# Normalised tokens of the later rounds made on VectorE instead of GpSimd, in both mixtures of experts

## What is computed

```python
x = w_norm * (xf * rsqrt(mean(xf * xf) + EPS))
logits = x @ w_router                    # 32 experts
w_topk, sel = top_k(softmax(logits), 4)
# each expert: up to 128 tokens in order; buf[e] = x[tok]
y = (silu(buf @ w_gate) * (buf @ w_up)) @ w_down
out[tok] += y[...] * w_topk
sh = sigmoid(x @ w_shared_gate) * (silu(x @ sw_gate) * (x @ sw_up) @ sw_down)
return inp + out + sh
```

## Time and profile before

| | |
|---|---|
| median of three runs | 2836.43 us (2834.74 to 2837.26) |
| profiled execution, its own time | 2849.46 us |
| span of the profiled execution | 2847.7 us |
| mean granted TensorE clock | 0.957 |
| busy: TensorE, VectorE, ScalarE, GpSimd | 92%, 65%, 45%, 30% |
| first mixture, from the start to the last marks | 1366 to 1536 us of the span |
| second mixture, the same stretch | 2457 to 2620 us |
| chain that ended last, by engine | TensorE 12%, VectorE 1%, DMA 1%, the rest under 1% |

### The profile page before, as it was taken

The page is one execution under the profiler, slowest core; times in us unless marked ns, Lnnn a source line. Parts: engine busy times, 40 slices in busy tenths (PEclk is TensorE's granted clock), DMA queues, the critical chain, the costliest instruction groups (busy, mean ns, idle before and its releaser), DMA issues. The chain is left out here.

```text
span 2847.7 us, 38702 instructions
## 1 busy us (share of the span) xinstructions
PE 2633.2 (92%) x14106; PEld 1258.1 (44%) x14106; DVE 1857.3 (65%) x3962; ACT 1268.9 (45%) x1936; POOL 850.1 (30%) x820
## 2 busy tenths in 40 slices
PE   4887999999999999788799998899999999899998
PEld 2443233333333332344465664344455454465665
DVE  6556988887877887366465334877767677366334
ACT  3332366656656667634221231255555555521221
POOL 2655032241331400166432441212111110153441
PEclk8897799999999999999899999799999999999999
DMA  3004312303303210000411663632334340301565
GB/s 122 1 1 99 51 36 39 62 18 56 60 20 51 43 26 2 1 1 1 141 34 39 146 156 97 122 55 54 57 63 63 62 68 2 111 17 50 124 161 156
DMA packets 162592, 175.76 MB, mean 62 GB/s; under 512 B 19090, under 2 KB 135762, under 8 KB 162258
## 3 DMA queue, kind: packets, MB, share of 16 engines
q1 hardware_dynamic: 146948, 152.57, 24.4%
q0 software_dynamic: 12416, 17.84, 3.8%
q10 hardware_dynamic: 3040, 2.88, 0.4%
HBM read 116.32 MB, written 56.13 MB: 61 GB/s over the span
## 5 line engine op out<-in xcount | busy, mean ns | idle before, releaser
L1853 DVE TENSOR_REDUCE a_mx<-a_bank 128x1 f32<-128x512 f32 (+3 forms) x1792 | 1035.6, 627 | 260.9 <-PE a_bank L1587 180.3
L1723 ACT ACTIVATE a_E<-a_bank 128x1024 f32<-128x1024 f32 (+3 forms) x896 | 796.0, 931 | 457.8 <-PE a_bank L1644 311.6
L1587 PE MATMUL a_bank<-a_KT,a_QT 96*128 96x512 bf16 (+4 forms) x1792 | 592.4, 376 | 26.6 <-DVE a_mx L1853 17.0
L1644 PE MATMUL a_bank<-a_QT,a_KT 99*128 99x512 bf16 (+4 forms) x1792 | 506.9, 358 | 4.2 <-DMA a_QT<-a_mT 2.3
L1659 PE MATMUL a_bank<-a_E,a_Vg 128*32 128x512 f32 (+3 forms) x3584 | 437.3, 560 | 0.7 <-ACT a_E L1723 0.7
L1587 PEld LDWEIGHTS a_bank<-a_KT,a_QT 96*128 96x128 bf16 (+1 forms) x1792 | 151.8, 98 | 516.5 <-DVE a_mx L1853 326.0
L1644 PEld LDWEIGHTS a_bank<-a_QT,a_KT 99*128 99x128 bf16 (+1 forms) x1792 | 170.3, 98 | 173.8 <-ACT a_E L1723 30.9
L1020 ACT ACTIVATE d_silu<-d_bank 128x512 f32<-128x512 f32 x96 | 57.2, 596 | 351.3 <-PE d_bank L894 345.6
L447 POOL TENSOR_TENSOR f_hl<-f_hT,f_hh 128x512 f16<-128x512 f32 x96 | 110.6, 1156 | 336.8 <-ACT f_hh L464 336.3
L1101 DVE SCALAR_TENSOR_TENSOR d_silu<-d_silu,d_bank 128x512 f32<-128x512 f32 x96 | 65.8, 685 | 202.7 <-ACT d_silu L1020 202.6
L909 PE MATMUL d_bank<-wdT,d_hT 128*128 128x256 f32 (+1 forms) x768 | 194.0, 396 | 4.2 <-DVE d_hT L1104 4.2
(11 more groups left out here) (243 smaller groups left out, 3775.6 us busy)
## 6 DMA issues: line engine op xcount, KB each, us to landing
parts<-a_parts SPq DMA_DIRECT2D x64, 384.0 KB, 2.6
a_QT<-parts SPq DMA_DIRECT2D x180, 128.0 KB, 5.7
a_KT<-parts SPq DMA_DIRECT2D x180, 128.0 KB, 8.9
d_wgu<-in_L_ffn_w_gate SPq DMA_DIRECT2D x64, 176.0 KB
d_wgu<-in_L_ffn_w_up SPq DMA_DIRECT2D x64, 176.0 KB
d_wd<-in_L_ffn_w_down SPq DMA_DIRECT2D x64, 176.0 KB
normalised<-d_xn SPq DMA_DIRECT2D x8, 1152.0 KB, 4.7
acc<-d_zero SPq DMA_DIRECT2D x2, 4224.0 KB, 15.8
```

Of the source, the lines that this page charges most:

```text
L1587: last = nc.tensor.matmul(out[:, 0:w], QT[0:W, h, qt * P:(qt + 1) * P], KT[0:W, h, kh * HALF:kh * HALF + w], start=True, stop=not diag)
L1644: last = nc.tensor.matmul(out, KT[:, h, kt * P:(kt + 1) * P], QT[:, h, half * HALF + c0:(half + 1) * HALF], start=True, stop=not diag)
L1723: nc.scalar.activation(E[:, u % 2, 2 * pair:2 * pair + 2, c0:HALF], bank[:, 2 * pair:2 * pair + 2, c0:HALF], ACT.Exp).then_inc(exps, 1)
L1853: nc.vector.tensor_reduce(mx[:, x[1] // C % 2, j, qt, kh:kh + 1], out[:, 0:w], AX.X, ALU.max).then_inc(freed_dve, 1)
```

## The change

The normalise function goes from GpSimd's program to VectorE's and takes the round as an argument; the two buffer waits go with it. Round 0 stays ahead of the slots. The tiles of round c + 1 are made in the slots of chunk c: tiles 0 to 2 in slot 1, 3 to 5 in slot 3, 6 and 7 in slot 4, each time behind the routing step of that slot and ahead of `spot`. GpSimd keeps `mark` alone. No sum or product changes.

```diff
@@ -787,15 +787,6 @@
                                                  in_=ys[:, e % 2, :], in_offset=None, compute_op=ALU.add,
                                                  bounds_check=NTOK + TRASH - 1, oob_is_err=True).then_inc(added, 16)
 
-                def normalise(r, i):
-
-                    t = r * RT + i
-                    if r > 1 and i == 0:
-                        pool.wait_ge(turned, START + (r - 1) * (RT // 2))
-                        pool.wait_ge(xn_sent[r % 2], START + 16 * (r // 2))
-                    nc.gpsimd.tensor_scalar(xn[:, r % 2, i, 0:D], core.x[:, t, :], core.mv[:, t, 0:1], both[:, t:t + 1],
-                                            ALU.subtract, ALU.mult).then_inc(normed, 1)
-
                 def mark(r):
 
                     pool.wait_ge(masked, START + r + 1)
@@ -807,18 +798,8 @@
                         last = nc.gpsimd.tensor_scalar(marks[:, 0, i], hot[:, i], core.const("token_hi")[:, t:t + 1], None, ALU.mult)
                     last.then_inc(marked, 1)
 
-                pool.wait_ge(normed, START + RT)
-                pool.wait_ge(scales, START + 5)
-                for i in range(RT):
-                    normalise(1, i)
                 for r in range(NS):
-                    if r + 2 < NS:
-                        for i in range(RT // 2):
-                            normalise(r + 2, i)
                     mark(r)
-                    if r + 2 < NS:
-                        for i in range(RT // 2, RT):
-                            normalise(r + 2, i)
                 pool.wait_ge(zeroed, START + 16 * 2)
                 for s in range(2):
                     pool.wait_ge(xn_sent[s], START + 16 * (NS // 2))
@@ -1087,9 +1068,13 @@
                 scale_step(nc.vector.reciprocal(both[:], both[:]))
                 scale_step(nc.vector.tensor_tensor(both[:], both[:], core.rstd[:], ALU.mult))
 
-                def normalise(i):
-
-                    nc.vector.tensor_scalar(xn[:, 0, i, 0:D], core.x[:, i, :], core.mv[:, i, 0:1], both[:, i:i + 1],
+                def normalise(r, i):
+
+                    t = r * RT + i
+                    if r > 1 and i == 0:
+                        dve.wait_ge(turned, START + (r - 1) * (RT // 2))
+                        dve.wait_ge(xn_sent[r % 2], START + 16 * (r // 2))
+                    nc.vector.tensor_scalar(xn[:, r % 2, i, 0:D], core.x[:, t, :], core.mv[:, t, 0:1], both[:, t:t + 1],
                                             ALU.subtract, ALU.mult).then_inc(normed, 1)
 
                 def hidden(c, j):
@@ -1234,7 +1219,7 @@
                     last.then_inc(stats, 1)
 
                 for i in range(RT):
-                    normalise(i)
+                    normalise(0, i)
                 nc.vector.memset(zero[:], 0.0).then_inc(cleared, 1)
                 scale_step(nc.vector.tensor_scalar(keep[:], core.rstd[:], 0.5, 1.0, ALU.mult, ALU.add))
                 scale_step(nc.vector.tensor_tensor(shift[:], core.rstd[:], core.mv[:, :, 0], ALU.mult))
@@ -1260,6 +1245,9 @@
                                 carry(c)
                         if j == 5:
                             locate(c)
+                    if c < NS - 1 and j in (1, 3, 4):
+                        for i in {1: (0, 1, 2), 3: (3, 4, 5), 4: (6, 7)}[j]:
+                            normalise(c + 1, i)
                     if 0 < c < NS and j in (0, 1):
                         spot(c - 1, j)
                     if c == NS - 1 and j == 5:
```

## The result

The changed kernel takes 2880.61 us (median of four runs, 2873.84 to 2882.6) against 2836.85 us for the kernel before (four runs): a ratio of 1.0152 with a 95% interval of 1.0133 to 1.0170, 43.8 us slower. Measured once more on another occasion (experiment e9) the ratio is 1.0123, interval 1.0101 to 1.0145. The forecast was 2868 us in a range of 2857 to 2881. The direction and the places of the waits were right, and the size stands at the very edge of the range. 2880.61 is held here against 2836.85; in e9 the kernel before had a median of 2841.09 us, so the change cost 35 to 44 us.

A forecast was written before the change was run, and what follows sets the result against it. TensorE was taken to bound the kernel, with GpSimd's normalising covered. Waits of 19.2 + 7.7 - 0.9 = 26.0 us plus 6 us of clock made 32 us on the 2836.43 us median: 2868 us, range 2857 to 2881.

The forecast's parts named there:

- What bounds: Both mixtures' dense slots: TensorE sets the pace, GpSimd's normalising is already covered; its removal gives only -0.9 us.
- Pair 1: Second transpose pair, slot 3: waits for the fourth tile behind the choice, 4.25, 2.68, 2.68 us per mixture, 19.2 in both.
- Pair 3: Last transpose pair: waits for tiles 6 and 7 behind mask, sums and carry, 1.28 us each, 7.7 us in all.
- the slow carry: VectorE's carry in slot 4 takes 0.60 us beside GpSimd's marks, assumed in every round, instead of 0.19.
- Sum of the waits: Both mixtures: 19.2 + 7.7 - 0.9 = 26.0 us of TensorE waiting, 23.5 with the fast carry.
- The clock: TensorE falling to a lower clock level after new waits: three falls at 2.1 us, +6 us, bounds -3 to 15.8.
- the whole-instruction lock: Rival: VectorE's carry waits out a whole GpSimd marks instruction, 11.3 us more, about 2880 us; chance 0.05.
- six falls and 2878 us: Rival: the clock falls after all six new pair 1 waits, 26.0 + 15.8, 2878 us; chance 0.08.
- swallowed mask wait: Rival: slot 5's present mask waits vanish into the new wait, 7.1 us less, 2855 us without clock; chance 0.09.
- Faster: Rival: GpSimd's normalising keeps TensorE's short waits and clock falls alive; 18.4 us loss goes, about 2817 us; chance 0.02.
- no change: Rival: the order does not come out as written, TensorE never waits, only 0.9 us is left; chance 0.02.
- doubled mode for fp32 tensor_scalar: Skill rule for VectorE's normalise: would shorten the pair 1 and pair 3 waits by 2 us in all; not adopted.

The follow-up runs named there:

- e9: The changed kernel unaltered, measured again on another occasion: 2879.53 us, ratio 1.0123 to the kernel before.
- e1: Changed kernel with the fourth tile normalised in slot 1 instead of slot 3: 2847.95 us, ratio 1.0030 to the kernel before.
- e2: Changed kernel with tiles 6 and 7 normalised in slot 3 instead of behind the carry in slot 4: 2862.77 us, ratio 1.0084.
- e5: Changed kernel with extra useless TensorE products ahead of pair 1's wait, four in round 1's transposes, two in rounds 2 and 3: 2871.61 us, ratio 1.0118.
- e4: Changed kernel with extra useless TensorE products ahead of pair 1's wait, eight in round 1's transposes, five in rounds 2 and 3: 2877.34 us, ratio 1.0151.
- e10: e6 with one more extra product ahead of each pair 1 wait (five in round 1's transposes, three in rounds 2 and 3): 2869.59 us, ratio 1.0097.
- e6: e5 with one extra product ahead of each pair 3 wait as well: 2873.0 us, ratio 1.0132.

## Why the prediction was right, and where it was off

**What bounds.** That TensorE sets the pace and that GpSimd's normalising was covered held: with it gone, the only wait on TensorE that got shorter is that for the mask of round 1, from 0.94 to 0.48 us, where 0.45 us off was forecast. The marks' wait stayed at 3.06 us, as forecast, since no normalise stood ahead of it.

**Pair 1.** Forecast 4.25 and 2.68 us of delay. From the row in front of them to the transposes it is 5.96 us (1386.69 to 1392.65) where it was 1.71, and in round 1 it is 5.63 where it was 2.97: 4.25 and 2.66 us. (The idle time is 4.08 and 2.60, as one product overlapped the next at the old place.) Right in both sizes, and e1 shows the cause: one tile moved ahead of the choice and the wait is gone.

**Pair 3.** Forecast 1.28 us with the slow carry, 0.87 with the fast one; measured 1.11 to 1.21 us of idle time in the first mixture (0.93 once in the second), 1.27 us in TensorE's starts in round 1, with the carry at 0.59 us in every round. Taking the slow carry was right, and e2 shows the cause.

**Sum of the waits.** 26.0 us forecast. The first part of span x clock is 24.0 us above the kernel before in e9; in the four runs of the result it is 2748.9 us, 24 to 25 above the kernel before on the other occasions. Right.

**The clock.** This is the term that was mis-sized: I took +6 us, and the second part rose by 12.5 us in e9 (by up to 17 if its 129 us are held against the groups of the other occasions). The step that failed is the count: "three falls at 2.1 us, the trace's own frequency". Both profiles of the changed kernel lose 11 to 13 us more inside the two mixtures than before, and both show it at the same six places: behind four of the six waits for pair 1 (rounds 0 and 1, not round 2), and in round 0 of both mixtures behind the mask and pair 3. That makes about 2 us a place, so the price of 2.1 us was right and the number was not.

The count went wrong twice. I held only new waits of over 2 us to be worth one. But behind the mask of round 0, where the kernel before has a fall in one mixture alone, the changed one has it in both, and for longer: the dense rows take 3.62 and 2.67 us. Pair 3's 1.21 us stand less than 1 us behind the mask's 2.12, with only the mask's small products between them. With either kind of wait alone the fall at this place is shorter (3.56 and 1.88 us in e2, 3.33 and 1.88 in e5, and alike in their second mixtures). The losses in the table point the same way: 4.1 us above the kernel before in e1 and 3.1 in e2, together less than the 11 to 13 of both kinds. That they strengthen each other is suggested by one profile of each, and not shown.

And the frequency, two of four, left out three waits of over 2 us in the trace of the kernel before, those for transfers at the start of the mixtures:

```profile
1369.83 3.67 PE L846 MATMUL d_bank<-consts,d_xn 128*128 128x128 f32 x16 [5.41 <-DMA d_wr<-in_L_ffn_w_shared_gate]
...
1377.03 3.78 PE L894 MATMUL d_bank<-d_xT,wgT 128*128 128x512 f32 x4 [3.53 <-DMA wdT<-in_L_ffn_sw_down]
...
2460.57 3.42 PE L846 MATMUL d_bank<-consts,d_xn 128*128 128x128 f32 x16 [6.34 <-DMA d_wr<-in_L_ffn_w_shared_gate]
```

Behind all three the granted clock was 0.50. Five of seven would have made four falls of six and 9 us, by my estimate, and 2871 us in all.

How much of the surplus hangs on TensorE being idle is shown in part: filling the waits took 8 to 14 us off the loss in the two mixtures in four traces, and the totals of e4 and e10 agree; those of e5 and e6 show less.

**The range and the nearest rivals.** The result lies 0.4 us inside the upper end of 2881, and that end has no sum behind it: 41.8 us of waits and six falls make 2878, half of the lock's 11.3 us on top would make 2884. That the time fell inside is luck in part. The rival nearest to the time, the whole-instruction lock with about 2880 us, is wrong: the carry of round 0 (1403.31) took 0.59 us beside a GpSimd instruction that ran from 1402.76 for 2.85. The next, six falls and 2878 us, had the number of places right, but named the six waits for pair 1, at a dearer price.

**The other rivals.** The swallowed mask wait is out: it is 2.12 us in round 0 as before. Faster and no change are out. The Trainium skill's doubled mode for fp32 tensor_scalar (VectorE: DVE Perf Modes, section on the perf-mode tier table) is not what runs here: the shortest of the 64 instructions is 398 ns, where the copy of as many elements takes 293.

**Open.** Part of the 43.8 us is the occasion: the ratio was 1.0152 once and 1.0123 once, and the clock's loss inside the mixtures accounts for 11 to 13 us beside some 24 of waits, 35 to 37 in all. The medians of the kernel before go from 2837.8 to 2841.2 us over the three later occasions, and that difference is in the second part.

## What to carry to other kernels

Before work is moved to an engine with room, look up for each piece who reads it next, and what stands ahead of it in the new queue: 0.41 us of work cost 4 us here because it was queued behind a step of the routing that itself hangs on the product just issued. The same instructions one to three slots earlier cost nothing. And price a new wait on TensorE at more than its length: the twelve waits here cost about half as much again in clock. When counting how often a wait is followed by a low clock, take in every wait of the trace, those for transfers too, and look at short waits that stand near others.

## What was not expected of the hardware

Span x clock is far steadier than the span: 2724.7, 2724.5 and 2723.7 us for the kernel before on three occasions, while single runs go from 2827 to 2852 us with granted clocks of 0.965 to 0.954. Keeping TensorE at useless products during waits gives back time even when the products overrun: e4 added 12.2 us of work, and its median of 2877.34 us is no worse than the changed kernel's 2879.53 and 2880.61. And TensorE went to the lower level, 1.2 GHz, without a wait in front too: in e10, behind the router's small products, 9 us after the last wait of over 1 us.
